# A scan of 512 Runge-Kutta steps on one core: where VectorE's loop turns, and the order of four side sums

## The reference

```python
def derivative(q, p, drive):
    i_couple = tanh(q) @ coupling.T                 # 8x1024 @ 1024x1024
    dq = q - q**3 / 3 - p + drive + i_couple + bias
    dp = EPSILON * (q + ALPHA - BETA * p)
# each step: four derivatives (RK4), each at a state made from the one before
q = clip(q + DT/6 * (dq1 + 2*dq2 + 2*dq3 + dq4), -20, 20)   # p likewise
# the output is x + q after every step
```

## Time and profile before

| | us |
|---|---|
| median of 3 runs | 5646.72 |
| lowest, highest | 5643.98, 5647.08 |
| the profiled execution's own time | 5647.13 |
| its span, first to last instruction | 5645.3 |

### The profile page before, as it was taken

The page is one execution under the profiler, slowest core; times in us unless marked ns, Lnnn a source line. Parts: engine busy times, 40 slices in busy tenths (PEclk is TensorE's granted clock), DMA queues, the critical chain, the costliest instruction groups (busy, mean ns, idle before and its releaser), DMA issues.

```text
span 5645.3 us, 584273 instructions
## 1 busy us (share of the span) xinstructions
PE 4394.8 (78%) x263627; PEld 3697.3 (65%) x263627; DVE 5124.9 (91%) x31055; ACT 2677.3 (47%) x12552; POOL 5.7 (0%) x16
## 2 busy tenths in 40 slices
PE   7887777777777777777777777777777777777777
PEld 3436666666666666666666666666666666666666
DVE  5569999999999999999999999999999999999999
ACT  3334444444444444444444444444444444444444
POOL 0000000000000000000000000000000000000000
PEclk9999999999999999999999999999999999999999
DMA  5100000000000000000000000000000000000000
GB/s 221 47 16 0 0 7 0 7 0 0 7 0 7 0 7 0 7 0 0 7 0 7 0 7 0 0 7 0 7 0 7 0 0 7 0 7 0 7 0 7
DMA packets 11597, 57.06 MB, mean 10 GB/s; under 512 B 2616, under 2 KB 2616, under 8 KB 8512
## 3 DMA queue, kind: packets, MB, share of 16 engines
q1 hardware_dynamic: 11056, 55.84, 2.5%
q10 hardware_dynamic: 528, 1.05, 0.1%
HBM read 40.11 MB, written 16.78 MB: 10 GB/s over the span
## 4 chain that ended last, share of the span: by engine, by line
DVE 48%; PE 35%; issue 13%; ACT 3%; DVEq 0%; DMA 0%; SPq 0%; ACTq 0%
PE ps L634 30%; DVE xb L675 23%; DVE tanh_parts L675 7%; DVE xb L835 6%; ACT xb L444 3%; DVE xb L855 2%; DVE drive L675 2%; DVE xb L963 2%; DVE xb L952 2%; PE ps L523 2%; DVE xb L959 1%; DVE xb L913 1%; PE ps L541 1%; PE ps L578 1%; PE ps L557 1%
## 5 line engine op out<-in xcount | busy, mean ns | idle before, releaser
L634 PE MATMUL ps<-coup,tanh_parts 128*16 128x96 f16 (+1 forms) x262272 | 4047.0, 220 | 1171.7 <-DVE tanh_parts L675 877.6
L634 PEld LDWEIGHTS ps<-coup,tanh_parts 128*16 128x16 f16 x262272 | 3536.9, 89 | 1682.4 <-DVE tanh_parts L675 1197.8
L675 DVE SCALAR_TENSOR_TENSOR xb<-xb 128x64 f32<-128x64 f32 (+2 forms) x17413 | 3006.7, 210 | 110.5 <-issue 75.3
L444 ACT ACTIVATE xb<-xb 128x24 f32<-128x24 f32 (+1 forms) x4098 | 940.7, 230 | 2352.3 <-DVE xb L675 2276.4
L835 DVE STREAM_TRANSPOSE xb<-ps 128x96 f32<-128x96 f32 (+1 forms) x4096 | 1285.6, 314 | 38.8 <-PE ps L634 0.6
L675 DVE SCALAR_TENSOR_TENSOR tanh_parts<-xb,tanh_parts 128x24 f16<-128x24 f32 (+1 forms) x4098 | 704.3, 172 | 192.0 <-ACT xb L444 169.9
L493 ACT ACTIVATE xb<-xb 128x64 f32<-128x64 f32 x2048 | 499.6, 244 | 64.2
L450 ACT ACTIVATE tanh_parts<-xb 128x24 f16<-128x24 f32 (+1 forms) x2050 | 470.8, 230 | 64.6
L855 DVE SCALAR_TENSOR_TENSOR xb<-xb 128x64 f32<-128x64 f32 x2049 | 451.2, 220 | 0.0
L462 ACT ACTIVATE tanh_parts<-xb 128x24 f16<-128x24 f32 (+1 forms) x2048 | 356.8, 221 | 121.0
L456 ACT ACTIVATE xb<-xb 128x64 f32<-128x64 f32 x1024 | 262.6, 256 | 95.5 <-DVE xb L675 95.4
(11 more groups left out here) (69 smaller groups left out, 715.3 us busy)
## 6 DMA issues: line engine op xcount, KB each, us to landing
xb<-in_x SPq DMA_DIRECT2D x8, 2048.0 KB, 8.1
drive<-in_x_pt SPq DMA_DIRECT2D x8, 2048.0 KB, 24.5
out_pt<-drive SPq DMA_DIRECT2D x16, 1024.0 KB, 4.7
drive<-in_coupling_t SPq DMA_DIRECT2D x8, 512.0 KB, 11.6
mask_v<-in_cond SPq DMA_DIRECT2D x8, 132.0 KB
probs<-in_wo ACTq DMA_DIRECT2D x1, 1024.0 KB, 5.6
w_qkv<-in_wq SPq DMA_DIRECT2D x1, 64.0 KB, 3.7
w_qkv<-in_wk SPq DMA_DIRECT2D x1, 64.0 KB, 5.3
```

Source lines behind the costliest of these rows:

```text
L444: nc.scalar.activation(cols(tanh_sb, CHUNKS[j]), cols(q, CHUNKS[j]), ACT.Tanh, scale=unit_of[1.0])\
L634: last = nc.tensor.matmul(product(s, j)[SQ * g:SQ * g + ROWS, :], tanh_parts[:, s % 2, k, :], coup[:, k, part, g, n0:n1, :].rearrange("p c ...
L675: return V.scalar_tensor_tensor(out=out, in0=a, scalar=factor, in1=c, op0=ALU.mult, op1=op1)
```

## The change

- VectorE's loop turns round behind `with_first_part` of stage 0 in place of behind `rest_of`: `forecast_third` and `with_first_part(1, ...)` go from `after_rest(0)` to the end of `until_rest(0)`.
- In the rest of `after_rest(0)`, `p_sum_g0` goes between `cubic_of` and `base_of`; `drive_step_of`, which stood there, goes to the tail of stage 3.
- In that tail `g0_of` goes behind `z_of_first`, which now has the wait for `side_ready` ahead of it, and `drive_step_of` takes the place of `q_sum_g0` between `cubic_of` and `base_of`.
- `q_sum_g0` goes to stage 0, behind `y_less_g0`, ahead of `rest_of` chunk 1.

The number of instructions in the loop is the same.

```diff
--- before.py
+++ after.py
@@ -922,9 +922,8 @@
                 axpy(forecast[:, :], less_q[:, :], 1 / 3, q_st[3][:, :]).then_inc(forecast_ready, 1)
 
 
-            def g0_of(now):
-
-                dve.wait_ge(side_ready, now)
+            def g0_of():
+
                 axpy(g0[:, :], p_st[:, :], -BETA, q_st[0][:, :])
 
             def p_sum_g0():
@@ -986,7 +985,7 @@
             base_of(0, 1)
             axpy(g0[:, :], p_st[:, :], -BETA, q_st[0][:, :]).then_inc(setup, 1)
             dve.wait_ge(setup, 11)
-            q_sum_g0()
+            drive_step_of(0)
 
 
             def until_rest(s, now_at, now):
@@ -1017,6 +1016,7 @@
                 q_of(s, 1, now)
                 if s == 0:
                     y_less_g0()
+                    q_sum_g0()
                 if s == 1:
                     q_sum_r1()
                 if s == 2:
@@ -1025,16 +1025,17 @@
                     drive_less_p(1 - now_at)
                     clip_q(made)
                 rest_of(parity, 1, made)
-                return made
-
-            def after_rest(s, now_at, made):
-
                 if s == 0:
+
                     forecast_third(made)
                     with_first_part(1, z_first_part, z2, made)
+                return made
+
+            def after_rest(s, now_at, made):
+
+                if s == 0:
+                    cubic_of(1, made)
                     p_sum_g0()
-                    cubic_of(1, made)
-                    drive_step_of(now_at)
                     base_of(1, made)
                 if s == 1:
                     with_first_part(2, z_first_part, z3, made)
@@ -1050,11 +1051,12 @@
                     p_next(made - 1)
                     base_of(3, made)
                 if s == 3:
-                    g0_of(made - 1)
+                    dve.wait_ge(side_ready, made - 1)
                     z_of_first()
+                    g0_of()
                     with_first_part(0, z_first_part, z, made)
                     cubic_of(0, made)
-                    q_sum_g0()
+                    drive_step_of(1 - now_at)
                     base_of(0, made)
 
             def after(now):
```

More of the change, by code:

```diff
@@ L1027, in until_rest @@
                 rest_of(parity, 1, made)
+                if s == 0:
+                    forecast_third(made)
+                    with_first_part(1, z_first_part, z2, made)
                 return made
@@ L1032, in after_rest @@
                 if s == 0:
-                    forecast_third(made)
-                    with_first_part(1, z_first_part, z2, made)
+                    cubic_of(1, made)
                     p_sum_g0()
-                    cubic_of(1, made)
-                    drive_step_of(now_at)
                     base_of(1, made)
```

## The result

The changed kernel takes 5565.27 us (median of 4 runs, 5563.29 to 5569.10) against 5646.90 before: ratio 0.9857, 95% interval 0.984 to 0.9874. The forecast was 5552, with a range of 5545 to 5574. The profiled execution took 5569.1 us, its span 5567.3.

The account below looks back on a forecast made before the run. Stages were taken as bound by a 2.49 us floor, with only those above it able to gain: 5647.1 - 74 (turn) - 20 (tail) = 5553, rounded to 5552 us; own range 5546 to 5561, stated range 5545 to 5574.

Parts of the forecast that it names:

- The floor: Each TensorE stage: product to chunk 1's turn, chunk 0's tanh rest, wake-up, 2.03 + 0.27 + 0.19 = 2.49 us at least.
- The turn: VectorE's loop turn in stage 0: two steps ahead cover it, gaining 0.29 us in each of 255 turns, 74 us.
- The forecast's early departure: Stage with the turn: the forecast leaves VectorE 0.38 us earlier for idle ScalarE, which can only help; no gain counted.
- The tail: Stage 3's tail on VectorE: 0.12 us shorter, of which 0.04 us count in each of 512 stages, 20 us.
- rival 4: Tail of stage 3: steps between dependent neighbours save nothing, only the turn's 74 us remain, 5573 us; chance 0.04.
- of 0.12 us only 0.04 are worth anything: Behind the tail: ScalarE's path would give TensorE's start at 3017.05, but the floor gives 3017.13, against 3017.17 before.
- rival 1: At the turn: handing over costs more or only one step fits, up to 0.13 us lost, 5560 to 5585; chance 0.11.
- rival 5: Stage ended by ScalarE stays 0.04 us above the floor for its own reason; turn as forecast, 5573 us; chance 0.03.
- What was moved at no cost: q_sum_g0 in stage 0 fits VectorE's 0.16 to 0.17 us idle before chunk 1's rest; drive_step_of replaces it in the tail.

Follow-up runs that it names:

- step_kept: The changed kernel with drive_step_of run a second time between p_sum_g0 and base_of of stage 0: 5568.66 us, ratio 0.9865.
- turn_three: The changed kernel with cubic_of also ahead of the loop's turn, three steps in all: 5602.90 us, ratio 0.9924.
- tail_back: The changed kernel with the old order of stage 3's tail (g0_of ahead of z_of_first): 5569.76 us, ratio 0.9867.
- turn_one: The changed kernel with only forecast_third ahead of the loop's turn and the first sum behind it: 5570.61 us, ratio 0.9869.

## Why the prediction was right, point by point

**The floor** held: TensorE's end, turn of chunk 1, rest of chunk 0. Once every stage starts on it, VectorE's instructions cost only where they pass it (step_kept).

**The turn**, 74 us in the sum, was right in size: the idle time of its stage fell from 0.82 to 0.52 us, 0.30 x 255 = 76. Handing two steps over cost nothing, where I took 0.07 us: the cubic starts 0.50 us after the rest. The branch stands 0.09 us behind the rest's start with two steps between them as with none (3019.98 against 3019.89, 3017.64 against 3017.55), so I take it that they had been handed over while the rest waited for its tanh. That agrees with the Trainium skill, "Perfetto Trace Analysis", section "Per-instruction lifecycle", by which a VectorE instruction is pushed into a wait queue and the sequencer goes on to decode. The register and branch instructions themselves did not pass an open wait in turn_three, as read there; the section does not say so.

**The forecast's early departure** was put at "can only help", which hid its size. With VectorE's order as changed, ScalarE's late `q_part` would have cost some 44 us. In the kernel before, VectorE's order made the turn of chunk 0 later by one more step, and the pair that waits for `q_part` took 0.35 us: there the two delays lay beside each other. The change removed both, which is why the sum came out. That was luck in part: the sum took the 0.63 us from turning chunk 0 to turning chunk 1 over from the earlier trace rows without asking whether `q_part` would be there in time. It was there because the forecast now stands ahead of the turn.

**The tail**, 20 us in the sum, is the term that was mis-sized: it measured 4 to 6, which the times alone do not tell from nothing, but 0.04 less 0.03 us in 512 stages is of that size. The mechanism in VectorE was right (0.62 to 0.49 us, chunk 0 turned earlier, the stage's start at the floor), and rival 4, by which VectorE would have saved nothing, did not hold: the tail is back at 0.62 us with the old order (tail_back). The step that failed is "of 0.12 us only 0.04 are worth anything": I took the next stage's length as given, and TensorE's end as 2.02 us after the start where it came at 2.05. A stage that starts 0.04 us earlier reaches its 49th matmul, the first that needs chunk 1, before ScalarE's copy of chunk 1 is there and waits 0.03 us. The kernel before showed this already: a stage with ScalarE's copy whose start ScalarE had not held back was 2.00 us long, the one that it had held back by 0.04 us was 1.96.

```profile
3012.12 2.00 PE L634 MATMUL ps<-coup,tanh_parts 128*16 128x96 f16 x128 [0.52 <-DVE tanh_parts L675]
```

The prediction read the two as one, "1.96 to 2.00 us". (The 2.00 of the earlier trace rows is another thing: the chain's piece for a stage that TensorE's timeline gives 1.97.) 5647 - 76 - 5 = 5566 is the sum with the two measured. The forecast's own range, 5546 to 5561, was missed by some 4 us; the stated range held through the room that it left for rivals 1, 4 and 5, and none of the three is what happened.

**What was moved at no cost** cost nothing that the trace shows: the waits ahead of the rest of chunk 1 fell from 1020 to 510, and that rest still starts 0.89 us behind the turning of chunk 1 (3019.00 to 3019.89; 3016.66 to 3017.55 before).

## What to carry to other kernels

In this kernel the loop's turn was hidden by steps ahead of it whose semaphores were already up, and a step that still waited was better put behind it; try both places. When a wait at a stage's start is shortened, look inside the stage for the next thing that was just in time, and look at the lengths of stages that started late against those that started early. When a step moves, follow what it releases on the other engines: here, with the new order, about half of what the turn's place was worth lay in ScalarE's queue.

## What the runs showed of the hardware

- VectorE's loop took 0.49 to 0.50 us from the start of the step behind which its branch ran to the first step behind the turn, with no step between the two or with one or two (3017.55 to 3018.05 before, 3019.89 to 3020.39 after, 3018.40 to 3018.90 in turn_one, 3016.00 to 3016.49 in turn_three).
- ScalarE starts a second, independent activation 0.14 us after the first (3005.27, 3005.41) and one that waits for the first 0.27 us after it (3019.62, 3019.89); so here a second tanh was done sooner than a copy of the first.
- VectorE's steps of 64 columns that do not depend on each other start 0.135 us apart; where the last two of three depended, the three took 0.62 us in place of 0.49 (tail_back against the changed kernel), and an independent step between the two cost nothing.
